# A cross network: x turned by two transposes of stacked blocks, and TensorE's waits carried by the products ahead of short groups

## The reference

```
x0 = xk = e                                   # (b, 39, 16)
for W in (f0, f1, f2):                        # 39*39, 128*39, 128*39 rows, 128 columns
    z   = einsum('bfd,bgd->bfgd', x0, xk)     # every pair of fields, by component
    cur = einsum('bpd,pm->bmd', z.reshape(b, -1, d), W)
    outs.append(cur); xk = cur
z = sum(concatenate(outs, 1), -1)             # (b, 384)
h = relu([z, dense_ctx] @ W_top1 + b_top1)    # 512
h = relu(h @ W_top2 + b_top2)                 # 256
y = h @ W_top3
```

## Time and profile before

| | |
|---|---|
| median of 3 runs (1269.62 to 1273.38) | 1272.41 us |
| the profiled execution | 1262.4 us |
| its span, first to last instruction | 1260.6 us |
| mean granted TensorE clock | 0.999 |
| TensorE products busy | 1230.0 us (98%), 6037 |
| TensorE weight loads busy | 1014.7 us (80%) |
| VectorE / ScalarE / GpSimd busy | 1080.0 / 983.5 / 964.8 us |
| chain that ended last | PE 94%, DVE 3%, issue 1% |

### The profile page before, as it was taken

How to read it: one execution, slowest core, us unless ns; L and a number is a source line. 1 busy time by engine, 2 the same in 40 slices (tenths; PEclk the granted TensorE clock), 3 DMA queues, 4 the chain that set the end, 5 groups by cost and what they waited for, 6 DMA issues and landing times.

```text
span 1260.6 us, 23302 instructions
## 1 busy us (share of the span) xinstructions
PE 1230.0 (98%) x6037; PEld 1014.7 (80%) x6037; DVE 1080.0 (86%) x3370; ACT 983.5 (78%) x3272; POOL 964.8 (77%) x745
## 2 busy tenths in 40 slices
PE   3999999999999999999999999999999999999998
PEld 2677788888888888888888888888888888888887
DVE  3889999789988899789997899978999789988884
ACT  2678887788877888778886888868888688877883
POOL 7788888688886788777887778867888678884462
PEclk9999999999999999999999999999999999999999
DMA  6484343323433323334331433313433223343000
GB/s 157 97 220 92 85 87 84 59 59 63 85 86 80 69 62 70 68 83 83 72 78 34 85 82 86 80 34 68 85 86 84 63 48 70 85 86 76 9 6 4
DMA packets 159563, 94.76 MB, mean 75 GB/s; under 512 B 114385, under 2 KB 122065, under 8 KB 159430
## 3 DMA queue, kind: packets, MB, share of 16 engines
q1 hardware_dynamic: 149190, 90.63, 32.5%
q0 software_dynamic: 10240, 2.64, 2.4%
HBM read 84.08 MB, written 3.87 MB: 70 GB/s over the span
## 4 chain that ended last, share of the span: by engine, by line
PE 94%; DVE 3%; issue 1%; POOL 1%; ACT 1%; DMA 0%; SPq 0%; DVEq 0%; ACTq 0%; POOLq 0%
PE pieces L867 23%; PE pieces L869 22%; PE pieces L868 22%; PE cur_bank L895 6%; PE cur_bank L851 4%; PE cur_bank L849 4%; PE cur_bank L850 3%; DVE parts L658 2%; PE gx_bank L883 1%; PE gx_bank L884 1%; PE gx_bank L885 1%; PE cur_bank L921 1%; PE gx_bank L821 1%; POOL emb L407 1%; PE pieces L938 1%
## 5 line engine op out<-in xcount | busy, mean ns | idle before, releaser
L481 ACT ACTIVATE parts<-pieces,x_cols 128x128 f32<-128x128 f32 x2560 | 723.5, 374 | 138.9 <-PE pieces L869 132.3
L658 DVE SCALAR_TENSOR_TENSOR parts<-pieces,x_cols,parts 128x128 f32<-128x128 f32 x2432 | 683.6, 344 | 139.8 <-PE pieces L869 118.5
L867 PE MATMUL pieces<-w_hi,cur_hi 128*128 128x512 f32 (+1 forms) x1280 | 514.8, 402 | 4.6 <-issue 2.4
L869 PE MATMUL pieces<-w_hi,cur_lo 128*128 128x512 f32 (+1 forms) x1280 | 498.5, 389 | 0.0
L868 PE MATMUL pieces<-w_lo,cur_hi 128*128 128x512 f32 (+1 forms) x1280 | 498.3, 389 | 0.0
L416 POOL TENSOR_TENSOR parts<-parts 128x1024 f32<-128x1024 f32 x127 | 305.4, 2404 | 159.7 <-DVE parts L658 156.9
L407 POOL DMA_INDIRECT emb<-in_table,rows x320 | 318.3, 995 | 81.8 <-issue 58.4
L867 PEld LDWEIGHTS pieces<-w_hi,cur_hi 128*128 128x128 f32 x1280 | 241.4, 189 | 56.5 <-DVE parts L658 6.8
L869 PEld LDWEIGHTS pieces<-w_hi,cur_lo 128*128 128x128 f32 x1280 | 240.9, 188 | 51.7
L868 PEld LDWEIGHTS pieces<-w_lo,cur_hi 128*128 128x128 f32 x1280 | 241.4, 189 | 40.0
L421 POOL TENSOR_TENSOR tails<-parts 128x512 f32<-128x512 f32 x127 | 164.2, 1293 | 18.1
(11 more groups left out here) (99 smaller groups left out, 835.6 us busy)
## 6 DMA issues: line engine op xcount, KB each, us to landing
partners<-x_wide SPq DMA_DIRECT2D x186, 234.0 KB
x_diag<-x_split SPq DMA_DIRECT2D x512, 10.0 KB
x_end<-x_wide SPq DMA_DIRECT2D x96, 80.0 KB
x_rep<-x_wide SPq DMA_DIRECT2D x96, 78.0 KB
partners<-x_wide SPq DMA_DIRECT2D x93, 80.0 KB
emb<-in_table,rows POOLq DMA_INDIRECT x320
partners<-x_wide SPq DMA_DIRECT2D x62, 66.0 KB
x_wide<-emb SPq DMA_DIRECT2D x32, 80.0 KB
```

The costliest lines, as they stand in the source:

```text
L481: last = nc.scalar.activation(parts[n % 2][:, 4 * i + r, :], src[:, r * H:(r + 1) * H], ACT.Copy, scale=x_cols[n // 4][:, n % 4, f:f + 1])
L658: nc.vector.scalar_tensor_tensor(acc, src[:, r * H:(r + 1) * H], x_cols[n // 4][:, n % 4, f:f + 1], acc, ALU.mult, ALU.add).then_inc(acc_d ...
L867: nc.tensor.matmul(dst[:, 0:width], hi[:, cols], w1_hi[:, ws], start=True, stop=False)
L869: nc.tensor.matmul(dst[:, 0:width], lo[:, cols], w1_hi[:, ws], start=False, stop=True).then_inc(l2d_ready if q in D_PIECES else l2a_ready, 1)
```

## The change

1. **x_stack.** A new tile of 117 rows by 256 columns holds x's column blocks 0, 1 and 2 one under the other (3 x 39 rows, 128 columns), and block 3 in the first 39 rows of the columns beside. SyncE fills it by four loads a tile (`load_stack`), behind `load_late` and ahead of the second half of `x_diag`; the first of them waits until the x before was turned. `transpose_x` becomes two transposes, of 117 and of 39 rows.
2. **Waits.** `layer2_piece` is split in three functions, one for each product, and the waits that stood before a short group are put before the second or third product of a piece ahead of it; the group's own first instruction keeps the wait that comes last.

```diff
+            def load_stack(tile):
+
+                wait(sp, transposed, tile)
+                first = x_wide[bass.ds(tile, 1), 0:F, :].rearrange("o r c -> (o r) c")
+                for r in range(REP):
+                    sp.dma_start(x_stack[r * F:(r + 1) * F, 0:P], first[:, r * P:(r + 1) * P]
+                                 ).then_inc(x_stack_loaded, 16)
+                sp.dma_start(x_stack[0:F, P:2 * P], first[:, REP * P:4 * P]).then_inc(x_stack_loaded, 16)
...
             def transpose_x(tile, i, gs):
 
-                pe.wait_ge(x_rep_loaded[i % 2], (tile - i % 2) * 8 * X_LOADS + 16 * X_LOADS)
-                wait(pe, x_cols_ready, tile)
                 wait(pe, g_copied, gs)
-                for j in range(4):
-                    last = nc.tensor.transpose(x_turns[j], x_rep[i % 2][0:F, j * P:(j + 1) * P], ident[0:F, 0:F])
-                last.then_inc(transposed, 1)
+                nc.tensor.transpose(x_turns[0], x_stack[:, 0:P], ident[0:REP * F, 0:REP * F])
+                nc.tensor.transpose(x_turns[1], x_stack[0:F, P:2 * P], ident[0:F, 0:F]).then_inc(transposed, 1)
...
             def sum_pairs(tile, i, k):
                 pe.wait_ge(pairs_lo_ready, g + 1)
-                if k == 0:
-                    wait(pe, cur1_lo_ready, tile)
-                    wait(pe, sum1_ready, tile)
-                    if i == 1:
-                        wait(pe, y_copied, tile // TILES - 1)
-                    if i == 2:
-                        wait(pe, l3_copied, tile // TILES)
...
+            def await_bank_read(tile, i):
+                if i == 1:
+                    wait(pe, y_copied, tile // TILES - 1)
+                if i == 2:
+                    wait(pe, l3_copied, tile // TILES)
+                if i == 3:
+                    wait(pe, h1_copied, tile // TILES * 2)
+                if i == TILES:
+                    wait(pe, h2_copied, tile // TILES - 1)
...
+                        layer2_first(u, n, q)
+
+                        if more and s == S_X - 1:
+                            pe.wait_ge(x_stack_loaded, (tile + 2) * (REP + 1) * 16)
+                        if more and s == steps.sum[0] - 1:
+                            await_last_sum(tile + 1)
+                        if g_next:
+                            await_diag(next_u - next_back, next_b)
+                        if g_now:
+                            pe.wait_ge(x_cols_ready, x_turned(u, at))
+                        if not first and at == S_L3[0] - 1:
+                            pe.wait_ge(g_copied, u * BLOCKS)
...
+                        layer2_second(n, q)
+
+                        if more and s == S_X - 1:
+                            pe.wait_ge(x_cols_ready, tile + 1)
+                        if more and s == steps.sum[0] - 1:
+                            await_bank_read(tile + 1, i + 1)
+                        if g_now:
+                            wait(pe, g_copied, (u - back) * BLOCKS + b)
...
+                        if more and tile > 0 and s == 4 * PIECES - 1:
+                            pe.wait_ge(cur1_lo_ready, tile + 2)
+                        layer2_third(n, q)
```

More of the change, by code:

```diff
@@ L172, in cin_kernel @@
         gx_bank = bank("gx_bank")
-        x_turns = [gx_bank[:, X_AT + j * F:X_AT + (j + 1) * F] for j in range(4)]
+        x_turns = [gx_bank[:, X_AT:X_AT + REP * F], gx_bank[:, X_AT + REP * F:X_AT + 4 * F]]
         h_sums = [cur1_bank[:, m * P:(m + 1) * P] for m in range(N1 // P)]
@@ L375, in quad @@
                         load_late(tile + 2, (i + 2) % TILES)
+                    if ahead:
+                        load_stack(tile + 2)
                     load_diag(tile, i, 1)
@@ L835, in sum_pairs @@
                 pe.wait_ge(pairs_lo_ready, g + 1)
-                if k == 0:
-                    wait(pe, cur1_lo_ready, tile)
-                    wait(pe, sum1_ready, tile)
-                    if i == 1:
-                        wait(pe, y_copied, tile // TILES - 1)
-                    if i == 2:
-                        wait(pe, l3_copied, tile // TILES)
-                    if i == 3:
-                        wait(pe, h1_copied, tile // TILES * 2)
-                    if i == TILES:
-                        wait(pe, h2_copied, tile // TILES - 1)
                 hi, lo = pairs_hi[buf][0:rows, :], pairs_lo[buf][0:rows, :]
@@ L852, in sum_pairs, with await_last_sum, piece_of, layer2_first @@
                                  ).then_inc(pairs_used, 1)
-            def layer2_piece(u, n, q):
-                width = min(4, F - 4 * q) * H
-                dst = pieces[(n * PIECES + q) % BANKS]
+            def await_last_sum(tile):
+                wait(pe, sum1_ready, tile)
+            def await_bank_read(tile, i):
[7 more added lines that the diff above has]
+                    wait(pe, h2_copied, tile // TILES - 1)
+            def piece_of(n, q):
+                width = min(4, F - 4 * q) * H
+                dst = pieces[(n * PIECES + q) % BANKS][:, 0:width]
+                lo, hi = cur1_lo[n // 4 % 2], cur1_hi[n // 4 % 2]
+                cols = slice(n % 4 * P, (n % 4 + 1) * P)
+                return dst, hi[:, cols], lo[:, cols], slice(4 * q * H, 4 * q * H + width)
+            def layer2_first(u, n, q):
                 g, back = (u * BLOCKS + n, q - BANKS) if q >= BANKS else (u * BLOCKS + n - 1, q - BANKS + PIECES)
@@ L879, in make_g @@
                     pe.wait_ge(x_diag_loaded[n // 2 % 2], (tile + 1) * 16 * DIAG_LOADS)
-                wait(pe, g_copied, g)
+            def make_g(u, n):
+                g = u * BLOCKS + n
+                pe.wait_ge(cur2_lo_ready, g + 1)
                 dst, hi, lo = gx_bank[:, 0:FX * BLK_B], cur2_hi[g % CURS][:], cur2_lo[g % CURS][:]
@@ L963, in quad @@
                         at = 4 * PIECES * i + s
-                        layer2_piece(u, n, q)
+                        steps = S_BEGIN if first and i == 0 else S_USUAL
+                        back, b = G_STEP.get(at, (0, 0))
+                        g_now = at in G_STEP and u >= back
+                        next_back, next_b = G_STEP.get((at + 1) % (BLOCKS * PIECES), (0, 0))
+                        next_u = u + (at + 1) // (BLOCKS * PIECES)
+                        g_next = (at + 1) % (BLOCKS * PIECES) in G_STEP and next_u >= next_back and next_u < QUADS
@@ new lines, in quad @@
+                        if not first and at == S_L3[0] - 1:
+                            pe.wait_ge(g_copied, u * BLOCKS)
+                        if not first and at == S_H1[0] - 1:
+                            pe.wait_ge(l3_copied, u)
+                        if not first and at == S_H2[0] - 1:
+                            pe.wait_ge(h1_copied, u * 2)
+                        if not first and at == S_Y - 1:
+                            pe.wait_ge(h2_copied, u)
+                        layer2_second(n, q)
@@ L965, in quad @@
+                        layer2_third(n, q)
                         if more and s == S_X:
                             transpose_x(tile + 1, (i + 1) % TILES, g_made(u, at))
-                        steps = S_BEGIN if first and i == 0 else S_USUAL
                         if more and s in steps.sum:
                             sum_pairs(tile + 1, i + 1, steps.sum.index(s))
-                        if at in G_STEP:
-                            back, b = G_STEP[at]
-                            if u >= back:
-                                make_g(u - back, b, x_turned(u, at))
+                        if g_now:
+                            make_g(u - back, b)
@@ L990, in _ @@
             pe.wait_ge(sum1_ready, QUADS * TILES)
-            make_g(u, BLOCKS - 4)
-            make_g(u, BLOCKS - 3)
-            make_g(u, BLOCKS - 2)
+            pe.wait_ge(x_cols_ready, QUADS * TILES)
+            for n in range(BLOCKS - 4, BLOCKS - 1):
+                await_diag(u, n)
+                pe.wait_ge(g_copied, u * BLOCKS + n)
+                make_g(u, n)
             warm_up(3, x_bank)
```

46 lines of the change are left out of this document (23 added, 23 removed).

## The result

| kernel | median us | runs | ratio to the kernel before |
|---|---|---|---|
| before | 1272.47 (1269.62 to 1274.17) | 10 | |
| changed | 1276.06 (1273.47 to 1279.11) | 10 | 1.0036 [1.0024, 1.0048] |

The changed kernel is slower by 3.6 us between the medians, 4.6 us by the ratio. The forecast was 5.1 us more, 1277.5. The ratio's interval lies on the bound of 0.3% that the prediction had set, above it with most of its length. Three executions that took far longer are left out of the ratios: 3122.15 us of the changed kernel here and, further down, 1514.95 us with the transposes alone and 4475.42 us with x_stack early.

A forecast was written before the change was run, and what follows sets the result against it. TensorE, busy 98% of the span, was taken to bound the kernel. Bank wait +8.9, group starts -1.4, transposes -2.5, start +0.1 gave +5.1 us: 1277.5 us, 0.40% more; range 1268 to 1285.

The forecast's parts named there:

- the bound of 0.3%: About 0.3%, 3.8 us, taken as what a measurement of this kernel tells from no change.
- The l3 wait on the third product of step 49: TensorE waits there for ScalarE's bank copy, 1.53 to 1.60 us; net 1.24 to 1.31 a quad, seven quads, 8.9 us lost.
- One sign: In the profile after, L891's weight load at step 49 waits for ScalarE's L544, some 1.1 us idle, seven times.
- The group starts: Third-layer and top-product starts, steps 39, 79, 119: no separate waiting instruction, 0.07 us x 21 = 1.4 us gained; bounds 0 and 2.9.
- L946, the one-column product: Last short group (L931 before): pause of 0.25 us in front and 0.2 behind with nothing late, left out of the sum.
- The transposes: 117- and 39-row pair replaces four 39-row transposes: 0.08 us gained, 31 times, 2.5 us; bounds 3.4 gained, 0.9 lost.
- SyncE's queue and the start: Four more loads a tile fit into SyncE's existing waits, nothing lost; at the start 0.1 us lost, bounds 0 and 0.5.
- the upper bound of +10.6: Sum of the terms' bounds on the slow side (9.2 + 0.9 + 0.5), 1283.0 us; low side +2.4, 1274.8.
- The base: Shown runs' median 1272.4 us is 10 above the profiled execution's 1262.4, unexplained; the forecast difference was laid on the median.
- Pauses made by waits: Rival: waits make the short groups' pauses, so carrying them ahead gains 18.6 against 8.9 lost, about -10 us, 1263; chance 0.10.
- Paid back in part: Rival: ScalarE and VectorE catch up during step 49's stop, later waits shrink, up to 3.4 us: +1.7, 1274; chance 0.20.
- The clock: Rival: the 1.5 us stop at step 49 drops TensorE's clock, seven quads losing 12 us more, 1289; chance 0.06.

The follow-up runs named there:

- x_stack early: Changed kernel with tile 1's four x_stack loads issued right behind its x_rep, ahead of its partners: ratios to the kernel before 1.0042 and 1.0037.
- group A: Four runs on one chip, kernel before 1262.31 us: l3 wait back 1.0033, transposes alone 1.0013, waits alone 1.0067, l3 wait back with 78-row transposes 0.9965.
- groups B and C: Later runs, kernels before 1271.59 and 1270.86 us: changed kernel repeated (1.0035, 1.0032), and variants with x_stack early, 78 rows or bank read first (0.9888 to 1.0042).

## Why the prediction came out

The forecast was right, and its large terms were right for the reasons given; one small term was wrong in kind, and was covered.

**The l3 wait on the third product of step 49.** Predicted 1.53 to 1.60 us of stop, net 1.24 to 1.31 a quad, 8.9 in all. The stop is 1.52, a hair under; less the 0.29 of the sum's first product, 1.23, or 8.6 us. Putting the wait back gives 8.4 in the loops, and moving the copy moves the stop by as much. One sign was off: the load was to be idle for some 1.1 us, and it was for 1.58; no row gives the 1.1.

**The group starts.** Predicted 0.07 each, 1.4 us. The pause went from 0.12 us, averaged over the 21 groups, to 0.06: 1.3 us. L946, the one-column product, kept its 1.7 us over seven times, as said. That the separate waiting instruction made the difference is the prediction's reading; the place agrees, and no run takes the instruction away alone.

**The transposes.** Predicted 0.08 us a tile, 2.5 us. Measured 0.07 in the group shown, 0.09 as the mean of the tiles of the loops, and 2.5 us over the 28 of them in the run with the transposes alone; the bound of 3.4 was not reached. The reading behind it, that a 39-row operand makes both pauses and a wait makes neither, was shown from both sides: the pauses stayed where the waits were carried ahead, and vanished with 78 rows. The Trainium skill's rule that a change of tiling mode drains the engine (TensorEngine Tiling (Array Packing), Key Properties) fits both (the next load comes 0.18 us after the 39-row one in the changed kernel, 0.07 after the second of 78 rows); no run here shows the mode itself. The 117-row transpose took 0.19 us up to the 39-row load, of which 0.10 is the pause in the rows of before; no run separates the two further.

**SyncE's queue and the start.** Predicted 0.1 us, bounds 0 and 0.5, from tile 0's first transpose alone, where 0.2 was seen. (The 2.6 us left for landing there forgot the 0.35 that x_rep's own last load takes to issue; some 2.3 were left.) The step that failed is the sentence "the data is asked for one tile later. Nothing." It holds for the loops, by the waits of 368.7 us that the queue has there. It was never applied to tile 1's loads, which are issued at the start behind all of that tile's partners and asked for at step 16 of tile 0. They cost 4.1 to 6.5 us in three profiles of group A, more than a third of that by the clock behind the wait. In groups B and C, and by its profile in the first measurement, the stop of all engines hid it. Without it the change would by these parts have cost 9 to 11 us, at the upper bound of +10.6 that the terms were summed to and twice the forecast: the forecast was also lucky here.

**The base.** "No row says why" the runs shown were 10 us above the profiled one: 8.8 of it is the stop near 40 us and the tail's clock. Laying the difference on the median was right for the time, but it hid that the start differed between executions, and so that a term at the start needed both cases.

**The rivals.** Pauses made by waits: refuted. Paid back in part: no; ScalarE's later waits did not shrink with the waits moved alone. The changed kernel's loops are +4.3 to +4.7 us against 5.0 summed, and the two halves of the change taken alone add up to 7.39 - 2.53 = 4.86. The clock: after 1.26 us of recorded idle at step 49 the granted clock stayed at 1.00. After 3.6 us in the first tile it fell to 0.5.

## What to carry to other kernels

A wait met long before costs nothing on the engine; so before moving one ahead, take from the timeline when its condition is met. A wait moved ahead of its condition stops all that stands between, and a producer that works off a queue of its own does not hurry. For a load that is added "one tile ahead", follow the first tile by itself: the prologue has neither the slack nor the order of the loop. And compare two profiles by the loops and the ends apart, since here a second profile of one kernel differed by 8.8 us, and its loops by 0.2.

## What the runs showed of the hardware

A weight load of 39 rows, or of one column, stands with a pause before it and one behind it; with 78, 117 and 120 rows there is none in front, and two transposes of 78 rows take 0.18 us with all around them (616.00 to 616.18) where four of 39 rows took 0.56 (0.79 less the 0.23 of the product in front). The group sum is what to look at, since the profile puts the pause on whichever load stands first.

The clock in the tail was not decided by the waits alone. The two profiles of the kernel before have the same waits there (1.35 and 1.36 us on L867); one stayed at the full clock and the other ran 3.4 us at half, for 1.57 us. The same holds near the start: each of the fourteen profiles has TensorE idle for 2.30 to 2.37 us at one and the same place (75.71 in the earlier trace rows), and behind it the clock fell to half in five of them and stayed full in nine.
